# Attention with a mixture of experts on one NeuronCore: minus the maxima written into the score banks by ScalarE, where a row product added them

## The reference, cut to what matters

```python
h = layernorm(x) * (1 + ca) + sa
c_q, c_kv = LN(h) @ w_down_q.T, LN(h) @ w_down_kv.T        # latents, 64 wide
q, k, v = per head (16 heads of 64) up projections of c_q, c_kv, c_kv; q, k rotated
attn = softmax(q @ k.T * 0.125)                            # per batch and head, 1024 x 1024
x = x + ga * ((attn @ v) @ w_out.T + h)
h = layernorm(x) * (1 + cb) + sb
x = x + gb * experts(h)                                    # 8 experts, the higher-numbered of the top 2
```

## Time and profile before

| | us |
|---|---|
| median of 3 runs (lowest, highest) | 905.26 (905.06, 907.29) |
| the profiled execution | 913.83 |
| its span, first to last instruction | 911.8 |
| TensorE matmuls busy in the span | 818.4 |
| VectorE, ScalarE, GpSimd busy | 636.7, 396.9, 663.3 |
| mean granted TensorE clock | 0.948 of full speed |

### The profile page before, as it was taken

The page is one execution under the profiler, slowest core; times in us unless marked ns, Lnnn a source line. Parts: engine busy times, 40 slices in busy tenths (PEclk is TensorE's granted clock), DMA queues, the critical chain, the costliest instruction groups (busy, mean ns, idle before and its releaser), DMA issues.

```text
span 911.8 us, 14689 instructions
## 1 busy us (share of the span) xinstructions
PE 818.4 (90%) x5118; PEld 490.1 (54%) x5118; DVE 636.7 (70%) x1156; ACT 396.9 (44%) x650; POOL 663.3 (73%) x348
## 2 busy tenths in 40 slices
PE   4668999999999999999999999999999977788671
PEld 2435555555555555555555555555555443377661
DVE  8957777777777777777777777777776757654112
ACT  3453544444444444444444444444444322345331
POOL 2386998989897878787878787878778845623323
PEclk8968999999999999999999999999999987979786
DMA  9000001010101010101011110101000000186763
GB/s 245 27 1 12 13 13 25 14 25 13 25 13 25 14 25 13 25 13 25 13 27 26 21 25 14 25 13 14 13 14 14 13 13 12 43 267 228 255 228 87
DMA packets 84329, 43.89 MB, mean 48 GB/s; under 512 B 57632, under 2 KB 73376, under 8 KB 84192
## 3 DMA queue, kind: packets, MB, share of 16 engines
q1 hardware_dynamic: 83232, 40.86, 17.6%
q0 software_dynamic: 1024, 2.10, 0.7%
HBM read 36.51 MB, written 6.16 MB: 47 GB/s over the span
## 4 chain that ended last, share of the span: by engine, by line
PE 80%; DVE 8%; issue 4%; POOL 3%; DMA 3%; ACT 1%; SPq 1%; another core or an unknown queue 0%; POOLq 0%; DVEq 0%; ACTq 0%
PE ps_o L456 25%; PE ps_m L422 9%; PE ps_x L410 8%; PE ps_s L440 7%; PE ps_s L446 6%; PE ps_s L442 6%; PE ps_s L444 6%; PE ps_s L473 3%; PE ps_s L464 3%; PE ps_s L591 2%; DMA moe<-xs_dram 2%; PE ps_s L600 1%; DVE mx L1104 1%; POOL xs_dram L960 1%; DVE hn L1193 1%
## 5 line engine op out<-in xcount | busy, mean ns | idle before, releaser
L946 POOL TENSOR_TENSOR acc<-acc,probs 128x1024 f32<-128x1024 f32 (+1 forms) x192 | 459.8, 2395 | 76.2 <-ACT probs L702 53.8
L1104 DVE TENSOR_REDUCE mx<-ps_m 128x2 f32<-128x1024 f32 x240 | 293.7, 1224 | 93.1 <-PE ps_m L422 92.6
L702 ACT ACTIVATE probs<-ps_s 128x1024 f32<-128x1024 f32 x256 | 248.9, 1024 | 163.2 <-PE ps_s L446 163.1
L456 PE MATMUL ps_o<-probs,c_all 128*64 128x512 f32 x1024 | 250.4, 610 | 0.0
L946 POOL TENSOR_TENSOR acc<-probs 128x1024 f32<-128x1024 f32 (+1 forms) x32 | 75.4, 2358 | 54.8 <-ACT probs L702 54.3
L440 PE MATMUL ps_s<-q_hi,k_hi 64*128 64x512 f32 x512 | 103.4, 400 | 12.0 <-DVE x_sb L1160 10.9
L456 PEld LDWEIGHTS ps_o<-probs,c_all 128*64 128x64 f32 x1024 | 62.6, 137 | 93.9 <-issue 44.6
L422 PE MATMUL ps_m<-k_hi,q_hi 64*128 64x512 f32 x480 | 108.0, 445 | 3.9 <-DVE mx L1104 3.9
L442 PE MATMUL ps_s<-q_hi,k_lo 64*128 64x512 f32 x512 | 101.8, 393 | 0.0
L446 PE MATMUL ps_s<-neg_row,one_row 64*128 64x512 f32 x512 | 101.7, 393 | 0.0
L444 PE MATMUL ps_s<-q_lo,k_hi 64*128 64x512 f32 x512 | 101.1, 391 | 0.0
(11 more groups left out here) (289 smaller groups left out, 1030.5 us busy)
## 6 DMA issues: line engine op xcount, KB each, us to landing
probs<-in_experts SPq DMA_DIRECT2D x15, 578.0 KB
rr<-rd_dram SPq DMA_DIRECT2D x62, 128.0 KB
wu<-in_wqk SPq DMA_DIRECT2D x16, 256.0 KB, 3.2
neg_row<-nm SPq DMA_DIRECT2D x256, 0.5 KB, 2.0
w_first<-in_experts SPq DMA_DIRECT2D x5, 578.0 KB
rot<-in_experts SPq DMA_DIRECT2D x5, 578.0 KB
hT<-in_experts SPq DMA_DIRECT2D x5, 578.0 KB
xs_dram<-zero SPq DMA_DIRECT2D x2, 960.0 KB, 7.4
```

The source lines that it names most:

```text
L456: ins = nc.tensor.matmul(ps_o[64 * h:64 * h + 64, :], c_all[:, (p // HP) * TB + kt, :], probs[:, st % 4, h, :], start=(kt == 0), stop=(kt ...
L702: nc.scalar.activation(probs[:, st % 4, :, :], ps_s[:, 2 * (st % 2):2 * (st % 2) + 2, :], ACT.Exp, scale=SCALE).then_inc(s["probs"], 1)
L946: V.tensor_tensor(acc[:, half, heads, :], first, probs[:, st % 4, heads, :], ALU.add).then_inc(s["added"], 1)
L1104: V.reduce_max(mx[:, :, kh, qt], max_banks(q, n), AX.X).then_inc(s["max_reduced"], 1)
```

## The change

Five edits go together:

- The row product (L446) and its tiles `one_row` and `neg_row` go. ScalarE writes minus the maxima into both banks of a step ahead of its products (`preset`), from `neg_wide`, which holds the row of a half on all 128 partitions. The first score product then adds to what is in the bank (start=False).
- TensorE waits for `preset` where it waited for `probs`, `row_placed`, `den_read` and `out_added`; these waits move to ScalarE.
- A maxima tile takes every fourth query of its half (`tile_queries`), so that `nm` holds four neighbouring queries in a partition. SP stores them to DRAM in one DMA and reads them back with two broadcasts to 128 partitions (`max_spread`).
- In groups 3 and 7 the second of the two value steps comes after the denominators and the output product.
- In SP's order the denominators' DMAs come ahead of the spread of the maxima.

```diff
-        one_row = sb("one_row", [P, P], F32R)
-        neg_row = sb("neg_row", [P, 2, S], F32R)
+        neg_wide = sb("neg_wide", [P, 2, 2, HALF])
...
+            half, t = divmod(qt, 4)
+            return slice(half * HALF + t, (half + 1) * HALF, 4)
...
-                    ins = nc.tensor.matmul(bank[:, h, :], q_hi[rows(h), q % 3, qt * P:(qt + 1) * P],
+                    ins = nc.tensor.matmul(bank[:, h, :], q_hi[rows(h), q % 3, tile_queries(qt)],
...
-                ge(pe, s["probs"], n_step(p, st) - 2)
-                if kt == 0:
-                    pe.wait_ge(row_placed[half], 128 * (p + 1))
-                if kt == 1:
-                    ge(pe, s["den_read"], n_part(p, half) - 2)
-                    ge(pe, s["out_added"], n_part(p, half) - 3)
+                pe.wait_ge(s["preset"], n_step(p, st))
...
-                for h in range(2):
-                    ins = nc.tensor.matmul(bank[h], one_row[rows(h), :], neg_row[rows(h), p % 2, qc], start=False, stop=True)
...
-                    for n in (2 * g - 2, 2 * g - 1):
+                    value_step(2 * g - 2)
                     if g in (3, 7):
                         pe.wait_ge(s["probs"], n_step(p, 2 * g + 1))
...
+                    value_step(2 * g - 1)
...
+            def preset(p, st):
+
+                half, kt = divmod(st, TB)
+                if p == 0 and st < 2:
+                    act.wait_ge(s["max_reduced"], NMAX - 1 + st)
+                ge(act, s["probs"], n_step(p, st) - 2)
+                if kt == 0:
+                    act.wait_ge(row_wide[half], 32 * (p + 1))
+                if kt == 1 and (p or half):
+                    ge(act, s["den_read"], n_part(p, half) - 2)
+                    nc.scalar.copy(ps_s[:, 2, :], neg_wide[:, half, 0, :])
+                    ge(act, s["out_added"], n_part(p, half) - 3)
+                    nc.scalar.copy(ps_s[:, 3, :], neg_wide[:, half, 1, :]).then_inc(s["preset"], 1)
+                else:
+                    nc.scalar.copy(ps_s[:, 2 * (st % 2):2 * (st % 2) + 2, :], neg_wide[:, half, :, :]).then_inc(s["preset"], 1)
...
                     expo(p, 2 * g)
                     expo(p, 2 * g + 1)
+                    if g < NGRP - 1:
+                        preset(p, 2 * g + 2)
+                        if g != 3:
+                            preset(p, 2 * g + 3)
+                    elif p < LAST:
+                        preset(p + 1, 0)
...
+                sp.dma_start(mr_dram[half].rearrange("h (p f) -> p h f", f=4), nm[:, half, :, :]).then_inc(row_out[half], 16)
+
+            def max_spread(q, half):
+
+                sp.wait_ge(row_out[half], 16 * (q + 1))
+                if q:
+                    sp.wait_ge(s["preset"], n_step(q - 1, TB * half + TB - 1))
                 for h in range(2):
+                    sp.dma_start(neg_wide[:, half, h, :],
+                                 mr_dram[half, h:h + 1, :].to_broadcast([P, HALF])).then_inc(row_wide[half], 16)
...
                 if p > 0:
+                    max_rows(p, 1)
                     den_cols(p - 1, 0)
                     inv_rows(p - 1, 0)
+                    max_spread(p, 1)
                     inv_spread(p - 1, 0)
```

More of the change, by code:

```diff
@@ L96, in build @@
         mx = sb("mx", [P, 2, 2, TB])
-        nm = sb("nm", [P, 2, 2, 4], F32R)
+        nm = sb("nm", [P, 2, 2, 4])
         den = sb("den", [P, HALF])
@@ L107, in build @@
         rt_sb = sb("rt_sb", [P, 12, TB * E])
+        mr_dram = nc.dram_tensor("mr_dram", [2, 2, HALF], F32, kind="Internal").ap()
         rd_dram = nc.dram_tensor("rd_dram", [2, 2, HALF], F32, kind="Internal").ap()
@@ L211, in build @@
             "max_row": "both heads' maxima of half the queries, negated (vector)",
-            "scores": "both heads' scores of a step, less the maximum (tensor)",
+            "preset": "a step's score banks hold minus the maximum (scalar)",
+            "scores": "both heads' scores of a step, added to it (tensor)",
             "probs": "their probabilities (scalar)",
@@ L250, in build @@
         up_in = sem("up_in")
-        row_placed = [sem(f"row_placed{n}") for n in range(2)]
+        row_out = [sem(f"row_out{n}") for n in range(2)]
+        row_wide = [sem(f"row_wide{n}") for n in range(2)]
         den_cols_in, inv_out, inv_in = sem("den_cols_in"), sem("inv_out"), sem("inv_in")
@@ L439, in score @@
                 for h in range(2):
-                    nc.tensor.matmul(bank[h], k_hi[rows(h), p % 3, kc], q_hi[rows(h), p % 3, qc], start=True, stop=False)
+                    nc.tensor.matmul(bank[h], k_hi[rows(h), p % 3, kc], q_hi[rows(h), p % 3, qc], start=False, stop=False, skip_group_check=True)
                 for h in range(2):
-                    nc.tensor.matmul(bank[h], k_lo[rows(h), p % 3, kc], q_hi[rows(h), p % 3, qc], start=False, stop=False)
+                    nc.tensor.matmul(bank[h], k_lo[rows(h), p % 3, kc], q_hi[rows(h), p % 3, qc], start=False, stop=False, skip_group_check=True)
                 for h in range(2):
-                    nc.tensor.matmul(bank[h], k_hi[rows(h), p % 3, kc], q_lo[rows(h), p % 3, qc], start=False, stop=False)
-                for h in range(2):
-                    ins = nc.tensor.matmul(bank[h], one_row[rows(h), :], neg_row[rows(h), p % 2, qc], start=False, stop=True)
+                    ins = nc.tensor.matmul(bank[h], k_hi[rows(h), p % 3, kc], q_lo[rows(h), p % 3, qc], start=False, stop=True, skip_group_check=True)
                 ins.then_inc(s["scores"], 1)
@@ L767, in exp_logits @@
                 nc.scalar.activation(rt[b][:, 1, :], rt[b][:, 0, :], ACT.Exp).then_inc(s["logit_exp"], 1)
+            preset(0, 0)
+            preset(0, 1)
             for p in range(NPAIR):
@@ L772, in _ @@
                         den_out(p - 1, 0, ps_s[:, 2, :])
+                        preset(p, 1)
                     if g == 4 and p > 0:
                         den_out(p - 1, 1, ps_s[:, 2, :])
+                    if g == 4:
+                        preset(p, 9)
                     if g == 6 and p == LAST:
@@ L1011, in then @@
                 dve.wait_ge(s["vector_step"], seq[0])
[L1013 to L1017, removed]
+            V.memset(ones[:], 1.0).then_inc(s["constants"], 1)
             def statistics(src, tiles):
@@ L1107, in neg_max @@
                 dve.wait_ge(s["max_reduced"], NMAX * q + TB * (half + 1))
-                ge(dve, row_placed[half], 128 * q)
+                ge(dve, row_out[half], 16 * q)
                 V.tensor_reduce(nm[:, half, :, :], mx[:, :, :, 4 * half:4 * half + 4].rearrange("p h k t -> p h t k"),
@@ L1437, in _ @@
             weights(2)
-            sp.wait_ge(s["constants"], 1)
-            max_rows(0, 0)
-            max_rows(0, 1)
+            for half in range(2):
+                max_rows(0, half)
+                max_spread(0, half)
             weights(3)
@@ L1454, in _ @@
                     inv_rows(p - 1, 1)
+                if p < LAST:
+                    max_spread(p + 1, 0)
+                if p > 0:
                     inv_spread(p - 1, 1)
```

13 lines of the change are left out of this document (4 added, 9 removed).

## The result

The changed kernel takes 919.52 us (median of 4 runs, 918.54 to 921.6), the kernel before beside it 905.98 (4 runs, 905.06 to 907.29): ratio 1.0154, 95% interval 1.0132 to 1.0175. It is 13.5 us slower; 914 was forecast. The profiled execution took 921.6, span 919.9, clock 0.948 as before. Beside the five edits the diff has three small ones that no run tried alone: the output product starts its accumulation only with its first part, a maxima tile waits for the last rotated unit of its half, and the memsets of the old row's tiles are gone.

The account below looks back on a forecast made before the run. TensorE was taken to bound the loop, with a hidden wait on VectorE's reduction through `ps_m`. Loads with row product +5, half boundaries +3, last pair +1 made +9 us on a 905.3 median: 914, range 889 to 930.

Parts of the forecast that it names:

- The row product: Attention-loop groups: removing the 512 matmuls of L446 gains 0.15 us a group, not 0.46; the rest waits behind the reduction.
- The skeleton U = S+2.34+2x: Time U of a group's first up product from group start S; x is the extra price of one stepped load.
- 18 us: Gain from removing the row product, over the 120 groups of the 15 pairs with maxima, instead of 55 us.
- The stepped load: Maxima load L422, step of 16 bytes: 0 to 0.10 us dearer, 0.096 taken; with the row product's gain +5 us.
- The presets: ScalarE's 256 bank writes: 0.97 to 1.26 us each, 1.02 taken; they fit in a group and cost nothing.
- Rival 3: ScalarE becomes the bound of the loop, with presets at 1.4 us: about 950 us; chance 0.07.
- Half boundaries: Moving a value step behind the output product adds one change of product kind, about 0.1 us, 30 times: +3 us.
- The sum: Whole kernel: +5 (stepped loads with the row product's gain) + 3 (half boundaries) + 1 (last pair) = +9 us.
- The DMA queue: SP's new stores and broadcasts cost nothing; `divide` waiting 1 to 2 us per half held below one chance in twenty.
- rival 2: VectorE's divide falls behind a GpSimd add, delaying the next reduction up to 1.7 us: about 960 us; chance 0.08.
- The last pair's +1: Pair without maxima: twice the second score step waits 0.5 us more, for a copy and hand-over behind `out_add`: +1 us.
- Rival 1: The stepped load is free, while divide waits some 0.2 us for GpSimd 28 times: 896 us (889 to 902); chance 0.35.

Follow-up runs that it names:

- e4: Kernel before without the row product L446 and nothing in its place (maxima made but not subtracted, exponential's scale divided by 64): 900.39 us, ratio 0.9883.
- e2: Kernel before, row product kept, with only the maxima tiles of every fourth query and the row placed to match: 929.27 us, ratio 1.0205.
- e7: Changed kernel with contiguous maxima tiles and its own store kept, so maxima land with other queries of the half: 893.23 us, ratio 0.9864.
- e3: Kernel before with only the second value step of groups 3 and 7 moved behind denominators and output product: 914.13 us, ratio 1.0041.
- e14: e11 with the second value step put back ahead of denominators and outputs at the half boundaries: 903.15 us, ratio 0.9905.
- e11: Changed kernel with contiguous tiles, maxima sent as 8 one-column DMAs into an SBUF row, then to DRAM and spread: 901.44 us, ratio 0.9876.
- e1: Changed kernel with contiguous maxima tiles and the maxima stored to DRAM as 4-byte pieces in one DMA: 982.85 us, ratio 1.0776.
- e8: Changed kernel with contiguous tiles, maxima stored to DRAM by 8 one-column DMAs behind the denominators' DMA: 1072.79 us, ratio 1.1875.
- e12: e11 with TensorE's first value step of a group moved in front of the second maxima: 944.99 us, ratio 1.0350.

## Why the prediction was right

1. *The row product is worth 0.15 us a group, not 0.46.* Right: 5.03 to 4.88 in e4. But under stepped loads its absence is worth still less, 5.17 (e2) to 5.13: there TensorE's own work puts the second maxima at S+2.08 and the wait puts them at S+2.01. And the loads cost 0.14 a group beside the row product (e2) and 0.25 without it (e7 to the changed kernel), where both are exposed. The skeleton U = S+2.34+2x gives 2.58 at the measured x of 0.122; measured 2.59. "18 us" was optimistic for the row product alone: e4 got 10.7, in part because groups 0 and 4 gain only when `out_add` has left its place (28 x 0.15 = 4 us); the rest is not traced.
2. *The stepped load*, "I take 0.096". This term was mis-sized: 306 - 184 = 122 ns, so the group's net is 0.24 - 0.15 = +0.09, measured +0.10, or +12 us for 120 groups in place of +5. It lies outside the bound of 0.10, which came from another engine's reads; that VectorE's price came so near TensorE's is luck, as no run here links the two. The sentence of the Trainium skill, page "SBUF — State Buffer", section Specifications (TRN2), on full bandwidth needing two hits in a line of 16 bytes, pointed the right way; the trace agrees with its direction, and the load is 1.66 times the unstepped one. The estimate beside it does not come out of this case's rows: half the pace of a load of 0.184 would be x = 0.18 and the sum 20 us higher, not 2 or 3.
3. *The presets cost nothing.* Right: 1029 ns each, and in the plain group nothing waits for one. ScalarE is busy for 79% of the stretch, where 85% was expected. Rival 3 is out.
4. *Half boundaries*, "about 0.1" for the added change of kind. A little more: 7.12 against 6.97 in e3, so 0.15 each, at most +4.5 us for all 30, and e3 alone measured +3.7 against the forecast's +3. "`out_add` no longer stands before the reduction, which changes nothing" is wrong once the row product is gone: e14 against e11 shows 0.26 a time. The sum was not hurt, because it had already credited groups 0 and 4 with the full 0.15.
5. *The DMA queue costs nothing, the divide stays quick.* Right for the changed kernel: the divide's mean is 795 ns (812 before). e1, e8 and e12 show how near the edge both are; of the 0.1 us that rival 2 saw to spare, the trace leaves about 0.03.
6. *The sum.* 120 x 0.10 + 30 x 0.15 = +16.5 us where I had +8. In the loop it is +14.8: only 27 of the 30 boundaries lie in it, and groups 0 and 4 and those of the last of the 15 pairs grew by less than 0.10. Measured in the ratio: +13.9, where the whole forecast was +9. The last pair's +1 was not measured alone.

Rival 1 (896) is refuted as a fact about the load, but its number was nearly what the change would have given with free loads: 893.

## What to carry to other kernels

A matmul that is taken away is worth only what the next event in its engine's order lets through: write down the wait that lies hidden under it before counting its time. A stepped read of TensorE's weights is a cost on the path wherever the load stands bare; move the step to a place where nobody waits, here into DMAs that write a row in SBUF. Before splitting a run of equal products in order to cover a wait, add up the switches: here 0.48 us against 0.39.

## What I had not expected of the hardware

- A weight load of 64x128 float32 with a step of 16 bytes: 306 ns (304 at the least) against 184.
- 1024 pieces of 4 bytes into DRAM: as one DMA (e1), they held the next small DMA back to 7.2 us where it takes 2.1; as 8 DMAs (e8), they landed 8.6 us after the last issue. With the same pieces into SBUF as 8 DMAs (e11), the denominators' way to the inverses' issue took 2.9 us.
- A step of value products on its own costs 0.32 us before it and 0.16 behind it, beside score products.
- The 128x512 divide on VectorE, 0.68 us at its quickest, takes 2.3 us in e12 (median, up to 2.85): it ends 0.55 us after the GpSimd add that was running when it started.
- In e1 and e8, at TensorE's waits of mostly 2 to 5 us, the granted clock fell to 1.2 GHz for 3.4 us and more, and eight value products took 3.68 us (e1) in place of 1.94; 28 and 56 us of the two losses lie there. In e12, which waits at every boundary too, the clock stayed full.
